# Six tiles of expert 0 take rows of 13 blocks instead of 14, and the last blocks' scatters and row loads move in GpSimd's and SyncE's order

## The reference

```python
x = x + attention(layernorm(x), ctx, ctx)      # 32 x 256 tokens of width 256, 16 heads of 16
xf = layernorm(x).reshape(-1, 256)             # 8192 tokens
scores = softmax(xf @ Wg.T)                    # 8 experts
expert_weights, expert_indices = top_k(scores, 2)
# for each token and each of its two experts e, weighted by expert_weights / their sum:
h1 = xf @ W1[e].T + (xf @ A1[e].T) @ B1[e].T + b1[e]    # hidden 512, rank 16
h3 = xf @ W3[e].T + (xf @ A3[e].T) @ B3[e].T + b3[e]
y_e = g @ W2[e].T + (g @ A2[e].T) @ B2[e].T + b2[e]     # g = silu(h1) * h3
x = x + sum of the weighted y_e
```

## Time and profile before

| | |
|---|---|
| time, median of 3 runs (lowest to highest) | 1360.52 us (1353.21 to 1363.71) |
| the profiled execution | 1362.29 us |
| its span, first to last instruction | 1360.5 us |
| TensorE matmuls busy | 1264.1 us (93%) |
| VectorE busy | 1056.2 us (78%) |
| ScalarE busy | 854.7 us (63%) |
| GpSimd busy | 525.4 us (39%) |
| mean granted clock of TensorE | 0.965 |
| the chain that ended last | PE 83%, DMA 4%, issue 4%, DVE 3%, ACT 2% |

### The profile page before, as it was taken

One profiled execution on the slowest core, in us unless ns is written; L12 is line 12 of the kernel. 1 busy time (PEld: TensorE's weight loads), 2 busy tenths in 40 slices (PEclk: granted clock), 3 DMA queues, 4 the chain that ended last, 5 costly groups with the idle time before them and its releaser, 6 DMA issues.

```text
span 1360.5 us, 35016 instructions
## 1 busy us (share of the span) xinstructions
PE 1264.1 (93%) x11835; PEld 974.4 (72%) x11878; DVE 1056.2 (78%) x3029; ACT 854.7 (63%) x1780; POOL 525.4 (39%) x710
## 2 busy tenths in 40 slices
PE   3699999999999999999987789999999999999997
PEld 1356666666666666666655668888888888888886
DVE  3668999999999999999765756767776777777665
ACT  4267777777777787777663535555555555555554
POOL 4012243444343444433323543443444444444444
PEclk9679999999999999999888989999999999999999
DMA  5678576676576676666444444444444445434343
GB/s 178 119 173 173 126 165 129 143 163 123 147 164 126 142 164 123 150 129 130 77 136 148 104 107 88 94 71 95 93 94 88 94 71 103 79 63 64 59 68 55
DMA packets 109136, 157.12 MB, mean 115 GB/s; under 512 B 17017, under 2 KB 90793, under 8 KB 104873
## 3 DMA queue, kind: packets, MB, share of 16 engines
q1 hardware_dynamic: 82818, 119.81, 39.4%
q0 software_dynamic: 26160, 35.28, 15.6%
HBM read 87.36 MB, written 67.04 MB: 113 GB/s over the span
## 4 chain that ended last, share of the span: by engine, by line
PE 83%; DMA 4%; issue 4%; DVE 3%; ACT 2%; SPq 2%; POOL 1%; POOLq 0%; ACTq 0%; DVEq 0%
PE pv_bank L789 9%; PE bank L80 9%; PE st_bank L773 8%; PE s_bank L758 8%; PE bank L81 8%; PE bank L79 7%; PE s_bank L79 4%; PE s_bank L81 4%; PE s_bank L80 4%; PE bank L679 2%; PE st_bank L1494 2%; PE pv_bank L79 2%; PE pv_bank L80 2%; PE pv_bank L81 2%; PE st_bank L80 2%
## 5 line engine op out<-in xcount | busy, mean ns | idle before, releaser
L995 DVE TENSOR_REDUCE maxes<-s_bank 128x2 f32<-128x512 f32 x512 | 346.2, 684 | 68.7 <-PE s_bank L758 62.1
L856 ACT ACTIVATE expo<-st_bank 128x512 f32<-128x512 f32 x512 | 300.9, 598 | 67.5 <-PE st_bank L773 65.5
L1472 POOL DMA_INDIRECT out_y<-y_out,f_token x138 | 215.2, 1560 | 25.9 <-issue 13.5
L758 PE MATMUL s_bank<-stack 65*128 65x256 bf16 x1024 | 202.2, 280 | 12.2 <-DVE maxes L995 6.8
L773 PE MATMUL st_bank<-stack 67*128 67x256 bf16 x1024 | 200.7, 278 | 2.6 <-ACT expo L856 2.5
L1471 POOL TENSOR_TENSOR f_hold<-ones 128x1 f32<-128x1 f32 x138 | 65.9, 478 | 321.7 <-ACT y_out L1632 321.6
L79 PE MATMUL s_bank<-xt_hi,stack 128*128 128x256 bf16 x600 | 164.3, 274 | 9.3 <-issue 6.2
L80 PE MATMUL s_bank<-xt_hi,stack 128*128 128x256 bf16 x600 | 164.1, 274 | 0.0
L81 PE MATMUL s_bank<-xt_lo,stack 128*128 128x256 bf16 x600 | 164.1, 274 | 0.0
L1632 ACT ACTIVATE y_out<-y_sum,gate 128x256 f32<-128x256 f32 x138 | 62.7, 500 | 160.6 <-DVE y_sum L1743 146.6
L1679 DVE SCALAR_TENSOR_TENSOR vals<-s_bank,b,vals 128x256 f32<-128x256 f32 x150 | 72.4, 484 | 114.5 <-ACT vals L1597 113.8
(11 more groups left out here) (228 smaller groups left out, 3037.6 us busy)
## 6 DMA issues: line engine op xcount, KB each, us to landing
stack<-qk_scratch SPq DMA_DIRECT2D x256, 128.0 KB, 5.5
rows<-expert_rows SPq DMA_DIRECT2D x64, 260.0 KB, 2.8
qk_scratch<-qk SPq DMA_DIRECT2D x32, 512.0 KB, 5.6
x<-in_x SPq DMA_DIRECT2D x16, 512.0 KB, 8.2
ctx_in<-in_ctx SPq DMA_DIRECT2D x16, 512.0 KB, 9.2
out_y<-x SPq DMA_DIRECT2D x32, 256.0 KB, 7.2
expo<-in_w_units SPq DMA_DIRECT2D x18, 256.0 KB
x<-in_w_units SPq DMA_DIRECT2D x18, 256.0 KB
```

Source lines behind the costliest of these rows:

```text
L758: ins = pe.matmul(s_bank[r % 2][:, n, :], stack[k][0:ROW_K, 0, h0 + n, a * P:(a + 1) * P], stack[k][0:ROW_K, 1, h0 + n, :], start=True, st ...
L856: act.activation(expo[:, s % E_RING], st_bank[s % 2][:], ACT.Exp, scale=SCALE).then_inc(exp_done, 1)
L995: dve.tensor_reduce(maxes[:, t, h0:h0 + 2], s_bank[r % 2][:], AX_X, ALU.max).then_inc(max_done, 1)
L1472: pool.indirect_dma_start(out=dram["y"], out_offset=bass.IndirectOffsetOnAxis(ap=token[:, a:a + 1], axis=0), in_=y_out[:, a, :], in_offset ...
```

## The change

The head tiles take the rows of blocks 0 to 12. `load_head` waits for those alone. The eight scatters of block 13 leave step 15's early slots and come behind `send_padding` and a wait for the head's loads, in slots 16 to 30. On VectorE `head_end` is taken one step earlier; the second half of block 15's moments with its scales goes from point (0, 4) to (1, 0), `weigh` from (2, 2) to (2, 3), `assign` (and `rank` on TensorE) from (2, 3) to (2, 4), and the table's last steps from (3, 2) to (3, 4). GpSimd issues three of block 15's scatters ahead of `send(2)` and the other five ahead of `send(3)`. SyncE waits for the last scatters after the table's DMA and two pads instead of before them; six pads, instead of seven, follow tile 6's load, and their completion is waited for at expert 1's first tile.

```diff
+LAST_SCATTERS = (16, 18, 20, 22, 24, 26, 28, 30)
             def load_head():
-                for p in range(NB - 2):
-                    if p >= NB - 2 - XR:
+                for p in range(NB - 3):
+                    if p >= NB - 3 - XR:
                         sp.wait_ge(x1_stored[p % XR], 32 * (p // XR + 1))
-                sp.wait_ge(scattered[(NB - 3) % 2], 16 * 2 * TT * (NB // 2 - 1))
-                sp.wait_ge(scattered[NB % 2], 16 * 2 * TT * (NB // 2 - 1))
+                for k in range(2):
+                    sp.wait_ge(scattered[k], 16 * 2 * TT * len(range(k, NB - 3, 2)))
...
-            for k in range(2):
-                sp.wait_ge(scattered[k], 16 * 2 * TT * (NB // 2))
-            rest()
+
+            def all_scattered():
+                for k in range(2):
+                    sp.wait_ge(scattered[k], 16 * 2 * TT * (NB // 2))
+
+            rest(all_scattered)
...
-                if 0 <= q - 2 < NB:
+                if 0 <= q - 2 < NB - 3:
                     slots_known(q - 2)
                     scatter_at(q - 2, (0, 1))
...
             send_padding()
             pool.wait_ge(rows_loaded, 16 * HEAD)
             pool.wait_ge(head_loaded, 16)
+            slots_known(NB - 3)
+            for i in range(2 * TT):
+                pool.wait_ge(st_ready, (NB - 1) * SLOTS + LAST_SCATTERS[i] + 1)
+                pause(1, i)
+                scatter(NB - 3, i)
             slots_known(NB - 2)
...
             scatter(NB - 2, 7)
+            slots_known(NB - 1)
+            for i in range(3):
+                scatter(NB - 1, i)
             send(2)
-            slots_known(NB - 1)
-            for i in range(4):
+            for i in range(3, 2 * TT):
                 scatter(NB - 1, i)
             send(3)
-            for i in range(4, 2 * TT):
-                scatter(NB - 1, i)
...
-                if (T, at) == (2, 3):
+                if (T, at) == (2, 4):
                     run(("rank", last, 0))
...
-                    if q == NB - 1 and u == 5:
-                        dve.wait_ge(gate_step, (NB - 2) * GATE)
+                    if q == NB - 2 and u == 5:
+                        dve.wait_ge(gate_step, (NB - 3) * GATE)
...
                 if (T, at) == (0, 4):
                     output(("out", last, 1))
+                if (T, at) == (1, 0):
                     dve.wait_ge(*free(("out", last, 1)))
                     moments("r", last, range(2, TT), False, True)
                     scales("r", last)
...
-                if (T, at) == (2, 2):
+                if (T, at) == (2, 3):
                     weigh(last)
-                if (T, at) == (2, 3):
+                if (T, at) == (2, 4):
                     assign(("rank", last, 0))
                 if (T, at) == (3, 1):
                     count_tiles()
                 if (T, at) == (3, 2):
+                    begin_tiles()
+                if (T, at) == (3, 4):
                     place_tiles()
...
         def early_rows(T, e, n):
+            if (e, n) == (1, 0):
+                sp.wait_ge(padded, 16 * (EXPERTS - 2))
             load_rows(T + 1)
...
-            pad(0, first_padded)
-            sp.wait_ge(first_padded, 16)
+            for e in range(2):
+                pad(e, first_padded)
+            sp.wait_ge(first_padded, 32)
             sp.wait_ge(row_loaded, 16)
+            all_scattered()
             load_rows(HEAD)
-            for e in range(1, EXPERTS):
+            for e in range(2, EXPERTS):
                 pad(e, padded)
-            sp.wait_ge(padded, 16 * (EXPERTS - 1))
             later_tiles(sp, early_rows, next_rows)
```

More of the change, by code:

```diff
@@ L1221, in count_tiles, with begin_tiles @@
                 table(dve.tensor_scalar(tiles_all[:], tiles[:], float(EARLY + 1), None, ALU.max), 7)
-            def place_tiles():
+            def begin_tiles():
                 shape = [P, EXPERTS + 1, EXPERTS]
@@ L1233, in place_tiles @@
                 table(dve.tensor_tensor(skip[:, 0:1], skip[:, 0:1], head_shift[:], ALU.subtract), 13)
+            def place_tiles():
                 shape = [P, EXPERTS]
@@ L1433, in early_rows, with rest @@
                 load_unit(e + 2, n)
-        def rest():
+        def rest(all_scattered):
             sp.wait_ge(table_ready, 3)
             sp.dma_start(at["tile_row"][0:1, :], at["tile_row_at"][:]).then_inc(row_loaded, 16)
-            pad(0, first_padded)
-            sp.wait_ge(first_padded, 16)
+            for e in range(2):
+                pad(e, first_padded)
+            sp.wait_ge(first_padded, 32)
             sp.wait_ge(row_loaded, 16)
+            all_scattered()
             load_rows(HEAD)
-            for e in range(1, EXPERTS):
+            for e in range(2, EXPERTS):
                 pad(e, padded)
-            sp.wait_ge(padded, 16 * (EXPERTS - 1))
             later_tiles(sp, early_rows, next_rows)
```

## The result

| | before | changed |
|---|---|---|
| median of 4 runs (lowest to highest) | 1356.87 us (1350.96 to 1363.71) | 1335.57 us (1334.28 to 1342.63) |
| span of the profiled execution | 1360.5 us | 1332.5 us |

The ratio is 0.985, with a 95% interval of 0.9812 to 0.9889. That is 20.4 us of 1356.87 (15 to 26 by the interval); the sum had 20.3. As a time, 1340 was forecast and 1335.57 measured: the forecast started from 1360.52, the median of three runs, and a fourth run of the kernel before, 1350.96, lowers that median to 1356.87.

The account below looks back on a forecast made before the run. TensorE, busy 93% of the span, bounds the kernel; losses are waits and half clock between 690 and 820 us. Terms 9.3 - 1.0 + 0 + 1.4 + 10.6 = 20.3 us take 1360.52 to 1340 us, range 1331 to 1350.

Parts of the forecast that it names:

- the sum: Whole change, attention's end through tile 7: 9.3 - 1.0 + 0 + 1.4 + 10.6 = 20.3 us saved.
- Head rows: Before tile 0's transposes: the 7.65 us wait goes, with 1.6 of half clock; 9.3 us saved (7.4 to 9.4).
- Block 13's scatters: GpSimd, slots 16 to 30: eight later scatters, landed by 724 us, delay nobody; 0.
- Moments: Tiles 0 and 1: tile 1's first product freed, norm up to 1.1 us later; loss 1.0 (1.2 gained to 3 lost).
- weigh, rank, assign: Tile 2: mask's wait goes, assign moves before y_sum; 0 (1.3 gained to 1.0 lost).
- Table: Tile 3: last steps move behind the halves, gaining 2.1 us, y_sum 0.6 late; 1.4 saved (0.5 to 2.1).
- Tile 6's and 7's rows: Tiles 5 and 6: waits for rows and half clock go, tiles fall to 9.20 and 8.29; 10.6 us saved.
- one sign that I had called one of being wrong: At tile 6: prediction is wrong if the table's row and pads, not the scatters, come last.
- Rival A: Head tiles fall to half clock all the same; saving 14 to 16 us, 1345; chance 0.18.
- B: Attention's end: half clock at 701 to 716 us (5 to 7 us) does not occur; 1334; chance 0.14.
- C: One gap stays, at tile 6 or the head load: 1350 (0.08), or no change, 1360 (0.03); chance 0.11.
- D: TensorE stays at half clock through the head, 7.5 us a tile; slower, 1370 with four tiles; chance 0.04.

Follow-up runs that it names:

- Head only: Kernel before with only the head's part added (13 blocks, block 13's scatters behind the head's loads); ratio to the kernel before 0.994.
- moments back: Changed kernel with block 15's moments and scales back at point (0, 4); ratio to the kernel before 0.9846.
- table back: Changed kernel with the table built in one piece at (3, 2) again; 92.3 us from attention's end to tile 7's first output, against 89.9.
- tail only: Kernel before with only SyncE's new order and GpSimd's new order for block 15 added; ratio to the kernel before 0.9925.
- second trace: Both kernels run once more, unchanged; spans 1352.8 us (before) and 1332.4 us (changed).
- head back: Changed kernel with only the head's part undone (14 blocks, block 13's scatters in step 15's early slots); ratio to the kernel before 0.9954.

## Why the prediction was right

*Head rows: 9.3 forecast.* From the last weighted sum to the halves behind the first product took 738.21 - 722.72 = 15.5 us before (line below) and 717.87 - 711.78 = 6.1 after: 9.4. Both terms held, the 7.65 of waiting and the 1.6 of clock. "Head only" gives 9.4 for tile 0 as well.

```profile
738.21 0.28 PE L79 MATMUL s_bank<-xt_hi,stack 128*128 128x256 bf16 x1
```

*Block 13's scatters: 0.* They began at 698.95 and 709.82, eight in 11.9 us, and nobody waited for them.

*Moments: -1.0 (from 1.2 gained to 3 lost).* Tile 0 gained 1.5 and tile 1 lost 4.2 against "moments back": a loss of 2.7, of which 1.5 is half clock in tile 1 and 1.2 is the place itself. That the stretch of "moments back" differs by only 1.1 is luck: it had half clock in tile 4 instead. The mechanism is as written: counted from the attention's end the norm comes at 22.2 us (733.96 - 711.78) instead of 21.1 in "moments back", the 1.1 forecast, and waits 2.47 (1 to 2.5 forecast). One reading was wrong: the 0.32 in the old trace was a wait of TensorE for ScalarE's rows, and not time to spare. `send(0)`, 2.4 us later, landed before it was needed.

*weigh, rank, assign: 0.* 12.5 us in tile 2 instead of 12.2: -0.3. The mask's 1.20 went, y_sum came later.

*Table: 1.4 (0.5 to 2.1).* Tile 3 fell by 1.4; "table back" gives 2.5 with tile 4, a part of it clock.

*Tile 6's and 7's rows: 10.6.* Tile 5 fell by 8.6 and tile 6 by 1.3; with "tail only" as measure, 10.2. I had tile 6 fall to tile 7's 8.29. It stays at 9.4 to 9.6 in every kernel without a wait for rows, with 1.2 to 1.4 us that the profile gives to "issue", on the way into the loop over later tiles; so 1.3 of the 2.60 were not the price of the wait for rows, and the term was that much too large. Tile 4 gave 0.6 that was not in the sum. The slack at tile 6 was 5.4 us (5.8 forecast). Ahead of it one sign that I had called one of being wrong came true: the two pads, not the scatters, came last (a wait of 2.0 us, 2.3 in the second trace). My own times said so, with the scatters landed by 787 and the pads by 789; it cost nothing, since the rows were in time.

*The sum.* 20.3 forecast, 18.2 in the stretch of the two first traces, 21.0 of the two second ones, 19.6 with both traces of before, 20.4 in the timed runs. That the last agrees to 0.1 us is luck: single stretches of the kernel before differ by 2.7. Rival A happened in part: half clock in tiles 1 and 3 of the changed kernel, about 1.5 us in the first and nothing in the other, below the 4 that I gave it. My reading of the old trace had missed one fall, from 780.9 to 784.3 us behind the wait of 3.53 in tile 3: four falls between 690 and 820 us, not three. It speaks against my ground for doubting A, that after 738 us the head's waits ran at full clock. B's condition was met in part in the profiled run: the fall in step 15 was 3 to 4 us long and there was none in step 14, and that run took 1334.28, B's 1334. It happened with either kernel, so the stretch, and not this time, tells what the change did. C and D did not occur. Of the Trainium skill's two rules in TensorE: Matmul & The Clock Gate, that on DMA waits ("HAM oscillation") decided at the head, where the clock stayed full; that on short idles ("A second HAM failure mode") fits tile 1 of the changed kernel, behind a wait of 2.47 us, but not of "head back", where the clock stayed full behind 2.46.

What stays open: why the attention's end varies by 11 us, and in particular when steps 14 and 15 fall to half clock. The fall in step 15 was long in 2 of 10 traces with 13 blocks in the head and in 2 of 4 with 14, that in step 14 was there in 4 of 10 and 3 of 4: too few to tell.

## What to carry to other kernels

When an engine waits for a DMA that waits for another engine's last small transfer, look for the share of the work that does not need that transfer: a block left out of the head cost nothing here, since the tiles' number was the same, and gave 9 us. Where two queues share one serial tail, cost them together: undoing either of them alone brought back nearly half the gap. Bulk writes that nobody needs soon still delay the small ones that somebody does, so place them by what lands beside them.

## What was not expected of the hardware

Seven writes of 260 KB issued within 8.1 us made a send of tile 4 land in 6.9 us instead of 3.8. And half clock did not follow from the length of a wait alone: behind the norm's wait of 2.46 to 2.47 us it came in both traces of the changed kernel, behind the same wait of 2.46 us in "head back" it did not.
